# Graph layer on one core: nine batches of edges fetched row by row on two queues, for three on one, with the own side in fp32

## The chip, the cores and the metric

The kernel runs on one core of a Trainium2 chip. The metric is the time of one execution in microseconds; a time stated for a kernel is the median of its runs. Engines are PE (matmul), DVE (VectorE), ACT (ScalarE), POOL (GpSimd) and SP (SyncE, which only issues transfers). ACT and POOL issue transfers of their own too; ACTq, SPq and POOLq in a row stand for such issuing work.

## The reference

A graph layer over 12,500 nodes of 128 features and 412,500 edges, sorted by `dst`, with a residual and a layer norm:

```
theta = x[dst] - x[src]
w = sigmoid(relu(theta @ W1 + b1) @ W2 + b2)
agg = segment_sum(w * theta, dst)
indeg = segment_sum(ones, dst)
out = layernorm(x + agg + indeg * (x @ W4 + b4))
```

## The kernel before

**Tiling.** Edges go through in batches of 7 x 128 (`BT` = 7, `BATCH` = 896), four batches to a chunk (`NB` = 4), 112 chunks, so 448 batches and one short last one. A chunk's edges all end in one window of 128 nodes. A prologue of about 195 us builds `table` in HBM, whose row for a node is 1 KB: `x @ W1` and `x` side by side; it also turns the lists of edges into `src_at` (the source of each edge, edge `p, t` of a batch in partition `p`) and `rel` (the node of the window to which it belongs).

**The source side.** For most batches POOL gathers the rows of `table` by an indirect DMA for each tile of 128 edges, seven a batch, into one of `RB` = 6 slots of `arena` (L783). 21 batches, the first of each fifth chunk, are *held*: POOL loads their rows of `x` in the prologue (L768) and PE projects them in small steps in the 20 batches before (L631, L644). Three batches are *fetched by hand*: `hand_row(g)` gives, from batch 40 on, one row `p` of 7 edges to each batch, ACT loads the 7 numbers into registers (L891) and issues 7 transfers of one 1 KB row each (L895) into `hand_x`. POOL gathers nothing for held and hand batches (24 of them) and goes straight on to the next of the other 425 (`ringed`). Before a batch it waits until its slot has been read (`scaled`) and until PE has done the own side of the batch two before.

**The own side.** PE forms `x[dst] @ W1 + b1` from the window: a one-hot matrix `hot_ne` (ACT: `away` L875, `hot_ne` L883) times the window's projection (L794). It works in bf16: the projection is split on DVE and ACT into three bf16 parts (`high` L910, `take_high` L1044, `mid` L914, `low` L1048), SP writes the parts to HBM (L672) and loads for each batch the 126 rows of 42 near nodes x 3 parts (`parts`, L666). In the prologue DVE works out where these 42 nodes lie (`near_lin`, `near_row`, `neg_ids`), with a round trip through HBM (`near_of`).

**A batch in the main loop.** DVE: `difference` (L998, subtracts the source side in PSUM), `weigh` (L1004), `one_hot_rows` (L1017), `add_logit` (L1012), `scale_rows` (L1027). ACT: `gate` (two sigmoids, L902, L904), the hand row, then `distance` and `one_hot` for batch g + 3. PE: `own_side(g + 2)`, then `add_up(g)` (7 matmuls of 128x130 fp32, L812), with small work in between. Once a chunk: `project_window` (L820), `take_window`, `take_sums`, `finish_rows`, `normalise`, and on SP `load_window` (L690, L691) and `store_result` (L699). The order is written by hand: each engine runs its own loop over the batches, and semaphores tie the loops together. The PSUM of the own side is double (`ps_z`), and the hot matrices and scaled rows are kept for `SB` = 3 batches.

## Time and profile before

| | |
|---|---|
| median of 3 runs | 3931.7 us (3930.0 to 3933.57) |
| the profiled execution | 3929.44 us, its span 3927.6 us |
| granted TensorE clock, mean | 0.619 of full speed |
| POOL busy | 2953.8 us, 75% |
| DVE busy | 2979.7 us, 76% |
| PE busy | 2018.4 us, 51% |
| ACT busy | 1255.4 us, 32% |
| DMA engines, mean busy share | about 0.5, 147 GB/s |

Busy time does not count the work of issuing: on POOL, an indirect DMA counts while its descriptors are written, and the gap to the next one does not; on ACT, register loads and transfers of single rows count as idle ("issue"); SP has no busy time at all. So the share of busy time says little here, and the gaps and what ends them say more.

### The profile page before, as it was taken

The page shows a single profiled execution, that of the slowest core. Times are in us where ns is not written, and L with a number is a line of the kernel's source. Part 1 is how long each engine was busy: PE and PEld are TensorE (multiplying, and loading weights), DVE is VectorE, ACT ScalarE, POOL GpSimd, SP SyncE. Part 2 cuts the span into 40 slices and gives each one's busy share as a digit, 9 for nine tenths or more (in the row PEclk, how much of TensorE's full clock was granted, in tenths as well). Part 3 has the DMA queues.
Part 4 walks back from the last instruction along what each step waited for, and adds up shares of the span by engine and source line. Part 5 has one row for each costly group of instructions (what it writes and reads, how often), then busy time and mean ns, then how long its engine had stood idle before and what let it go on. Part 6 is the DMA issues. An engine that isn't in the chain of part 4 may idle for free.

```text
span 3927.6 us, 48444 instructions
## 1 busy us (share of the span) xinstructions
PE 2018.4 (51%) x10531; PEld 1781.0 (45%) x10531; DVE 2979.7 (76%) x4855; ACT 1255.4 (32%) x2220; POOL 2953.8 (75%) x3123
## 2 busy tenths in 40 slices
PE   3245555555545555555555555555555555555554
PEld 2244444444444444444444444444444444444444
DVE  7568777777777777777777777778778777777777
ACT  1223333333333333333333333333333333333332
POOL 7777777777777777777777777777777777777776
PEclk5565665566666556665666656666666665665666
DMA  7445455555555555555555545555555555555553
GB/s 234 131 138 148 144 147 143 146 147 147 147 147 147 147 147 148 146 148 147 147 147 143 148 145 147 147 146 148 148 146 147 147 148 145 146 148 144 149 147 105
DMA packets 343028, 577.99 MB, mean 147 GB/s; under 512 B 127642, under 2 KB 216768, under 8 KB 342501
## 3 DMA queue, kind: packets, MB, share of 16 engines
q0 software_dynamic: 147264, 399.12, 36.0%
q10 hardware_dynamic: 49501, 110.40, 8.7%
q1 hardware_dynamic: 145970, 65.36, 6.2%
q8 instruction: 87, 1.43, 0.1%
q14 instruction: 206, 1.69, 0.1%
HBM read 549.00 MB, written 31.99 MB: 148 GB/s over the span
## 4 chain that ended last, share of the span: by engine, by line
POOL 60%; issue 24%; DVE 8%; ACTq 4%; ACT 2%; DMA 1%; PE 0%; POOLq 0%; DVEq 0%
POOL arena L783 56%; POOL held_x L768 4%; ACTq L895 3%; DVE logit L1012 2%; DVE diff L1004 2%; DVE ps_both L998 1%; DMA arena<-table,lists 1%; ACT away L875 1%; ACTq L891 1%; DVE edge_rows L1027 1%; DVE edge_rows L1017 1%; ACT hot_ne L883 0%; ACT ps_log L902 0%; DVE square L976 0%; DVE rstd L978 0%
## 5 line engine op out<-in xcount | busy, mean ns | idle before, releaser
L783 POOL DMA_INDIRECT arena<-table,lists x2970 | 2810.2, 946 | 905.0 <-issue 899.5
L875 ACT ACTIVATE away<-dst_rows,neg_ids 126x896 bf16<-126x896 bf16 (+1 forms) x449 | 466.4, 1039 | 1587.6 <-issue 1587.6
L812 PE MATMUL ps_win<-edge_rows 128*128 128x130 f32 x3140 | 716.3, 416 | 424.7 <-DVE edge_rows L1027 406.7
L812 PE MATMUL ps_sum<-edge_rows 128*128 128x130 f32 x3136 | 713.4, 415 | 422.2 <-DVE edge_rows L1027 404.3
L812 PEld LDWEIGHTS ps_win<-edge_rows 128*128 128x128 f32 x3140 | 663.2, 319 | 482.8 <-issue 482.6
L812 PEld LDWEIGHTS ps_sum<-edge_rows 128*128 128x128 f32 x3136 | 660.1, 318 | 480.2 <-issue 479.6
L998 DVE TENSOR_TENSOR ps_both<-ps_both,arena 128x896 f32<-128x896 f32 x425 | 467.0, 1099 | 485.6 <-DMA arena<-table,lists 482.0
L794 PE MATMUL ps_both<-parts,hot_ne 126*128 126x128 bf16 x3138 | 334.3, 266 | 958.7 <-ACT hot_ne L883 633.7
L794 PEld LDWEIGHTS ps_both<-parts,hot_ne 126*128 126x128 bf16 x3138 | 245.9, 118 | 1072.1 <-issue 569.7
L1027 DVE TENSOR_TENSOR edge_rows<-arena,ps_log 128x896 f32<-128x896 f32 x425 | 461.5, 1086 | 129.2 <-ACT ps_log L902 129.0
L1004 DVE SCALAR_TENSOR_TENSOR diff<-ps_both,w_rows 128x896 f32<-128x896 f32 (+1 forms) x449 | 489.4, 1090 | 15.4
L1017 DVE TENSOR_TENSOR edge_rows<-ps_log,lists 128x896 f32<-128x896 f32 (+1 forms) x449 | 484.8, 1080 | 0.0
L1012 DVE TENSOR_REDUCE logit<-diff 128x7 f32<-128x896 f32 (+1 forms) x449 | 482.3, 1074 | 0.0
L883 ACT ACTIVATE hot_ne<-away,ones_col 126x896 bf16<-126x896 bf16 (+1 forms) x449 | 467.1, 1040 | 43.2 <-ACT away L875 1.5
L902 ACT ACTIVATE ps_log<-logit,b_col 128x7 f32<-128x7 f32 (+1 forms) x449 | 120.4, 268 | 900.1 <-DVE logit L1012 899.6
L768 POOL DMA_INDIRECT held_x<-in_x,held_at x147 | 143.1, 973 | 50.0 <-issue 47.6
L1048 DVE TENSOR_TENSOR stage<-rest,stage 128x128 bf16<-128x128 f32 x112 | 32.8, 292 | 167.2 <-ACT stage L914 166.8
L904 ACT ACTIVATE edge_rows<-logit,b_col 128x7 f32<-128x7 f32 (+1 forms) x449 | 130.8, 291 | 0.1
L976 DVE SCALAR_TENSOR_TENSOR square<-rstd,neg_half 128x1 f32<-128x1 f32 x336 | 74.5, 222 | 12.0
L644 PE MATMUL ps_hid<-w,held_xT 128*128 128x128 f32 x294 | 71.4, 383 | 0.0
L644 PEld LDWEIGHTS ps_hid<-w,held_xT 128*128 128x128 f32 x294 | 66.5, 306 | 0.0
L978 DVE SCALAR_TENSOR_TENSOR rstd<-square,rstd 128x1 f32<-128x1 f32 x336 | 54.1, 161 | 11.5
(136 smaller groups left out, 1198.6 us busy)
## 6 DMA issues: line engine op xcount, KB each, us to landing
dst_rows<-rel_of ACTq DMA_DIRECT2D x224, 441.0 KB
arena<-table,lists POOLq DMA_INDIRECT x2970
held_x<-table ACTq DMA_DIRECT2D x2688, 1.0 KB
parts<-parts_of SPq DMA_DIRECT2D x449, 31.5 KB
parts_of<-stage SPq DMA_DIRECT2D x112, 96.0 KB, 3.4
winT<-in_x_cols SPq DMA_DIRECT2D x112, 64.0 KB
window<-in_x SPq DMA_DIRECT2D x112, 64.0 KB
out<-yout SPq DMA_DIRECT2D x112, 64.0 KB
```

Source lines behind the costliest of these rows:

```text
L644: last = nc.tensor.matmul(ps_hid[:, (2 + t) * P:(3 + t) * P], held_xT[:, t, :], w14[:, 0:F], start=True, stop=True)
L768: nc.gpsimd.indirect_dma_start(held_x[:, h * BT + t, :], None, x, ids).then_inc(held_in, 16)
L783: nc.gpsimd.indirect_dma_start(gath[:, slot_of(g) + t, :], None, table, ids)\
L794: last = nc.tensor.matmul(ps_z[b][:, t, :], hot_ne[0:WK, b, t * P:(t + 1) * P], parts[0:WK, buf, :], start=True, stop=True)
L812: last = nc.tensor.matmul(ps_sums(c), hot_en[:, b, t, :], scaled_x[:, b, t, :], start=(j == 0 and t == 0), stop=(stop and t == tiles_of(g) ...
L875: nc.scalar.activation(away[0:WK, b, 0:n], dst_rows[0:WK, p % 2, lo:lo + n], ACT.Abs, bias=neg_ids[0:WK, near_no(g):near_no(g) + 1]).then_ ...
L883: nc.scalar.activation(hot_ne[0:WK, b, 0:n], away[0:WK, b, 0:n], ACT.Relu, bias=ones_col[0:WK, :], scale=-1.0).then_inc(hot_ready, 1)
L998: v.tensor_tensor(ps_z[b][:, 0:n, :], ps_z[b][:, 0:n, :], u, ALU.subtract).then_inc(z_read, 1)
L1004: v.scalar_tensor_tensor(diff[:, 0:n, :], ps_z[b][:, 0:n, :], 0.0, w2_rows[:, :].rearrange("p (a f) -> p a f", a=1).to_broadcast([P, n, F] ...
L1012: v.tensor_reduce(logit[:, b, 0:n], diff[:, 0:n, :], AX.X, ALU.add).then_inc(logit_ready, 1)
L1017: v.tensor_tensor(hot_en[:, b, 0:n, :], ps_col.rearrange("p (a n) -> p a n", a=1).to_broadcast([P, n, P]), rel[:, lo:lo + n].rearrange("p ...
L1027: v.tensor_tensor(scaled_x[:, g % SB, 0:n, 0:F], rows, ps_wgt(g).rearrange("p (t a) -> p t a", a=1).to_broadcast([P, n, F]), ALU.mult)\
```

## The change

Three things, which the diff shows in this order.

1. **Nine hand batches.** Batches 92, 135, 178, ... 436 (`92 + 43 m`) are fetched row by row, for 170, 301 and 432. The numbers of a hand batch are first written to HBM (`hand_of`) and loaded as one row of 896 into partition 0 (`hand_at`, two buffers). SP takes edges 0 to 594 of each such batch, 56 in a chunk, in two runs of 28, each with one register load; ACT takes the other 301, 7 a batch in all of the 387 batches from 42 on, in three pieces (2, 2 and 3) ahead of, between and behind `distance` and `one_hot`. `hand_x` becomes double. So POOL gathers 419 batches, for 425.
2. **Windows two chunks ahead.** SP's turn `c` starts when `finish_rows(c - 2)` is done and loads the window of chunk `c + 2`. `window` gets 4 buffers, `winT` 3. Results are stored in turn `c` for chunk `c - 2`. On PE `project_window(c + 2)` moves from the third to the fourth batch of chunk `c`, on DVE `take_window` from there to the first batch of the next chunk.
3. **Own side in fp32.** `hot_ne` and `own` are fp32 and of all 128 nodes; the splitting, `parts`, `near_*` and all that belongs to them go.

```diff
-HAND = 3
-HAND_FROM = 40
+HAND = 9
+HAND_FROM = 42
+SPAN = 43
+ACT_EACH = 7
+SP_ROWS = BATCH - ACT_EACH * SPAN
+SP_FROM = -(-HAND_FROM // NB)
+SP_LOAD = 28
+SP_EACH = 2 * SP_LOAD
 EARLY = 3
 FULL = CHUNK + 102
...
-        self.hand = [HAND_FROM + (P + 2) * (m + 1) + m for m in range(HAND)]
-        assert self.hand[-1] < self.batches and HAND_FROM > self.held[1] and not set(self.hand) & set(self.held)
+        self.hand = [HAND_FROM + SPAN * (m + 1) + 2 * NB - 1 for m in range(HAND)]
+        assert self.hand[-1] < self.batches and not set(self.hand) & set(self.held)
+        assert HAND_FROM > self.held[1] and HAND_FROM + SPAN > self.held[3] and SP_EACH * SPAN >= SP_ROWS * NB and\
+            SP_FROM + -(-HAND * SP_ROWS // SP_EACH) < self.chunks
...
         def hand_row(g):
-            for m, at in enumerate(z.hand):
-                row = g - (z.hand[m - 1] + 2 if m else HAND_FROM)
-                if g < at:
-                    return (m, row) if 0 <= row < P else None
-            return None
+            m, n = divmod(g - HAND_FROM, SPAN)
+            return (m, SP_ROWS + n * ACT_EACH) if 0 <= m < HAND else None
+
+        def sync_rows(c):
+            lo = (c - SP_FROM) * SP_EACH
+            runs = []
+            for m, row in [divmod(n, SP_ROWS) for n in range(lo, lo + SP_EACH) if 0 <= n < HAND * SP_ROWS]:
+                if runs and runs[-1][0] == m and runs[-1][2] < SP_LOAD:
+                    runs[-1][2] += 1
+                else:
+                    runs.append([m, row, 1])
+            return runs
+
+        def hand_free(m):
+            return (z.hand[m - 2] if m >= 2 else z.held[2 * m + 1]) + 1
+
+        def hand_numbers(kind, m, row, n):
+            return nc.values_load_multi_w_load_instructions(
+                hand_at[0:1, m % 2, row:row + n], engines=[kind], min_val=0, max_val=z.nodes - 1,
+                skip_runtime_bounds_check_because="src holds numbers of nodes")[1]
+
+        def hand_transfer(eng, m, row, number):
+            p, t = divmod(row, BT)
+            eng.dma_start(hand_x[p:p + 1, m % 2, t, :], table[bass.ds(number, 1), :])\
+                .then_inc(hand_in[2 * m + row % 2], 16)
 
...
-        def load_parts(sp, g, row):
-            buf = g % (2 * NB)
-            sp.dma_start(parts[0:WK, buf, :], parts_of[chunk_of(g) % SLOTS, bass.ds(row, WK), :])\
-                .then_inc(parts_in[buf], 16)
-
...
+        def load_window(sp, c, base):
+            sp.dma_start(winT[:, c % 3, :], x_cols[:, bass.ds(base, P)]).then_inc(window_in[c % 4], 16)
+            sp.dma_start(window[:, c % 4, :], x[bass.ds(base, P), :]).then_inc(window_in[c % 4], 16)
+
...
             sp.wait_ge(y_ready, c + 1)
             if c:
                 sp.wait_ge(y_out[(c - 1) % 2], 16 * ((c - 1) // 2 + 1))
             sp.sem_inc(sp_gate, 1)
-            base = clamped(base_i, c, c + 1, z.last_base)[0]
             sp.dma_start(out[bass.ds(base, P), :], yout[:, c % 2, :]).then_inc(y_out[c % 2], 16)
+
+        def store_numbers(sp):
+            sp.wait_ge(src_ready, 1)
+            sp.sem_inc(sp_gate, 1)
+            for m, g in enumerate(z.hand):
+                lo = first_tile(g)
+                sp.dma_start(hand_of[m, :].rearrange("(p t) -> p t", t=BT), src_at[:, lo:lo + BT])\
+                    .then_inc(hand_of_out, 16)
+            sp.wait_ge(hand_of_out, 16 * HAND)
+            sp.sem_inc(sp_gate, 1)
+            for m in range(2):
+                load_numbers(sp, m)
+
+        def load_numbers(sp, m):
+            if m >= 2:
+                sp.wait_ge(scaled, hand_free(m))
+                sp.sem_inc(sp_gate, 1)
+            sp.dma_start(hand_at[0:1, m % 2, :], hand_of[m:m + 1, :]).then_inc(hand_at_in[m % 2], 16)
+
+        def fetch_by_sync(sp, m, row, n):
+            if row == 0:
+                sp.wait_ge(scaled, hand_free(m))
+                sp.wait_ge(hand_at_in[m % 2], 16 * (m // 2 + 1))
+                sp.sem_inc(sp_gate, 1)
+            for k, number in enumerate(hand_numbers(mybir.EngineType.SP, m, row, n)):
+                hand_transfer(sp, m, row + k, number)
 
...
-            for c in range(last_chunk + 1):
-                if c < last_chunk:
-                    store_parts(sp, c + 1)
-                if c:
-                    store_result(sp, c - 1)
-            store_result(sp, last_chunk)
+            store_numbers(sp)
+            for c in range(1, last_chunk):
+                wait(sp, rows_done, c - 1)
+                sp.wait_ge(win_ready, c)
+                sp.sem_inc(sp_gate, 1)
+                lo, hi = max(c - 2, 0), min(c + 2, last_chunk)
+                bases = dict(zip(range(lo, hi + 1), clamped(base_i, lo, hi + 1, z.last_base)))
+                if c + 2 <= last_chunk:
+                    load_window(sp, c + 2, bases[c + 2])
+                for m in range(2, HAND):
+                    if c == hand_free(m) // NB + 2:
+                        load_numbers(sp, m)
+                rows = sync_rows(c)
+                for m, row, n in rows[:1]:
+                    fetch_by_sync(sp, m, row, n)
+                if c >= 2:
+                    store_result(sp, c - 2, bases[c - 2])
+                for m, row, n in rows[1:]:
+                    fetch_by_sync(sp, m, row, n)
+            bases = clamped(base_i, last_chunk - 2, last_chunk + 1, z.last_base)
+            for c in range(last_chunk - 2, last_chunk + 1):
+                store_result(sp, c, bases[c - last_chunk + 2])
             for q in range(2):
                 sp.wait_ge(y_out[q], 16 * len(range(q, last_chunk + 1, 2)))
...
             def own_side(g):
-                b, buf = g % 2, g % (2 * NB)
+                b, c = g % 2, chunk_of(g)
                 wait(pe, relu_ready, g - 1)
-                pe.wait_ge(parts_in[buf], 16 * (g // (2 * NB) + 1))
+                pe.wait_ge(own_ready, c + 1)
                 pe.wait_ge(hot_ready, g + 1)
                 for t in range(tiles_of(g)):
-                    last = nc.tensor.matmul(ps_z[b][:, t, :], hot_ne[0:WK, b, t * P:(t + 1) * P],
-                                            parts[0:WK, buf, :], start=True, stop=True)
+                    last = nc.tensor.matmul(ps_z[b][:, t, :], hot_ne[:, b, t * P:(t + 1) * P], own[:, c % 2, :],
+                                            start=True, stop=True)
                 last.then_inc(z_ready, 1)
 
...
@@ -846,7 +828,7 @@
                 c, j = chunk_and_place(g)
                 if g + 2 < all_batches:
                     own_side(g + 2)
-                if j == 2 and c + 2 <= last_chunk:
+                if j == 3 and c + 2 <= last_chunk:
                     project_window(c + 2)
                 add_up(g)
                 if j == 1 and c:
...
-                nc.scalar.activation(hot_ne[0:WK, b, 0:n], away[0:WK, b, 0:n], ACT.Relu, bias=ones_col[0:WK, :],
+                nc.scalar.activation(hot_ne[:, b, 0:n], away[:, b, 0:n], ACT.Relu, bias=ones_col[:, :],
                                      scale=-1.0).then_inc(hot_ready, 1)
 
-            def fetch_hand(m, row):
-                if row == 0:
-                    act.wait_ge(scaled, (z.hand[m - 1] if m else z.held[1]) + 1)
+            def load_hand(m, row):
+                if row == SP_ROWS:
+                    act.wait_ge(scaled, hand_free(m))
+                    act.wait_ge(hand_at_in[m % 2], 16 * (m // 2 + 1))
                     act.sem_inc(act_gate, 1)
-                lo = first_tile(z.hand[m])
-                ids = nc.values_load_multi_w_load_instructions(
-                    src_at[row:row + 1, lo:lo + BT], engines=[mybir.EngineType.Activation], min_val=0,
-                    max_val=z.nodes - 1, skip_runtime_bounds_check_because="src holds numbers of nodes")[1]
-                for t in range(BT):
-                    nc.scalar.dma_start(hand_x[row:row + 1, t, :], table[bass.ds(ids[t], 1), :])\
-                        .then_inc(hand_in[2 * m + t % 2], 16)
+                return hand_numbers(mybir.EngineType.Activation, m, row, ACT_EACH)
+
+            def fetch_hand(m, row, numbers, part):
+                lo, hi = part * ACT_EACH // 3, (part + 1) * ACT_EACH // 3
+                for k in range(lo, hi):
+                    hand_transfer(nc.scalar, m, row + k, numbers[k])
 
...
-                    mid(c + 1)
                 gate(g)
-                if g == 0:
-                    high(1)
-                if j == 3 and c + 2 <= last_chunk:
-                    high(c + 2)
-                if hand_row(g):
-                    fetch_hand(*hand_row(g))
+                by_hand = hand_row(g)
+                if by_hand:
+                    numbers = load_hand(*by_hand)
+                    fetch_hand(*by_hand, numbers, 0)
                 if g + 3 < all_batches:
                     distance(g + 3)
+                if by_hand:
+                    fetch_hand(*by_hand, numbers, 1)
+                if g + 3 < all_batches:
                     one_hot(g + 3)
+                if by_hand:
+                    fetch_hand(*by_hand, numbers, 2)
                 if g % DB == 0 and g + 3 + DB < all_batches:
...
             def take_window(c):
                 dve.wait_ge(win_ready, c + 1)
-                wait(dve, low_ready, c)
-                v.tensor_tensor(own[:, :], ps_window(c)[:, 0:F], b1_rows[:, :], ALU.add).then_inc(own_ready, 1)
+                v.tensor_tensor(own[:, c % 2, :], ps_window(c)[:, 0:F], b1_rows[:, :], ALU.add).then_inc(own_ready, 1)
                 wait(dve, rows_done, c - 2)
                 v.tensor_tensor(lin[:, c % 3, :], ps_window(c)[:, F:2 * F], b4_rows[:, :], ALU.add).then_inc(win_read, 1)
-
-            def take_high(c):
-                dve.wait_ge(high_ready, c + 1)
-                v.tensor_tensor(rest[:, :], own[:, :], stage[:, c % 2, 0, :], ALU.subtract).then_inc(rest_ready, 1)
-
-            def low(c):
-                dve.wait_ge(mid_ready, c + 1)
-                v.tensor_tensor(stage[:, c % 2, 2, :], rest[:, :], stage[:, c % 2, 1, :], ALU.subtract)\
-                    .then_inc(low_ready, 1)
 
...
                 difference(g)
                 weigh(g)
-                if j == 1 and c < last_chunk:
-                    low(c + 1)
                 one_hot_rows(g)
                 add_logit(g)
                 if g == 0:
                     take_window(1)
-                if j == 3 and c + 2 <= last_chunk:
-                    take_window(c + 2)
+                if j == 0 and 0 < c < last_chunk:
+                    take_window(c + 1)
                 if j == 1 and c:
                     take_sums(c - 1)
                 scale_rows(g)
-                if j == 0 and c < last_chunk:
-                    take_high(c + 1)
                 if j == 1 and c:
                     finish_rows(c - 1)
                 if j == 2 and c:
@@ -1147,13 +1097,10 @@
```

In the order of the instructions the change shows at three places. SP, one turn of its loop, of before (about chunk 50; `held_x<-table` is a transfer of one row, as `hand_x` lies in the memory of `held_x`):

```order
L672 DMA parts_of<-stage 128x384 [waits low_ready]
L660 TENSOR_LOAD base_i [waits rows_done,win_ready]
L690 REGISTER_ALU
L690 DMA winT<-in_x_cols 128x128
L691 ISA
L691 DMA window<-in_x 128x128
L660 TENSOR_LOAD near_row [waits parts_out0]
L666 ISA
L666 DMA parts<-parts_of 126x128
...
L660 TENSOR_LOAD base_i [waits y_ready,y_out1]
L699 ISA
L699 DMA out<-yout 128x128
```

SP, one turn of its loop, of the change:

```order
L636 TENSOR_LOAD base_i [waits rows_done,win_ready]
L641 REGISTER_ALU
L641 DMA winT<-in_x_cols 128x128
L642 ISA
L642 DMA window<-in_x 128x128
L443 TENSOR_LOAD hand_at
L449 ISA
L449 DMA held_x<-table 1x256
...
L649 ISA [waits y_ready,y_out1]
L649 DMA out<-yout 128x128
L443 TENSOR_LOAD hand_at
```

The pair of lines L449 stands 28 times behind each load of `hand_at`: 56 transfers of a row take the place of the write of the parts and of four loads of parts.

ACT, one batch of before:

```order
L902 ACTIVATE ps_log<-logit,b_col 128x7 [waits logit_ready,summed]
L904 ACTIVATE edge_rows<-logit,b_col 128x7
L891 TENSOR_LOAD lists
L895 ISA
L895 DMA held_x<-table 1x256
...
L875 ACTIVATE away<-dst_rows,neg_ids 126x896 [waits rows_of_dst_in1,hot_ready]
L883 ACTIVATE hot_ne<-away,ones_col 126x896 [waits away_ready,z_ready]
```

ACT, one batch of the change:

```order
L884 ACTIVATE ps_log<-logit,b_col 128x7 [waits logit_ready,summed]
L886 ACTIVATE edge_rows<-logit,b_col 128x7
L443 TENSOR_LOAD hand_at
L449 ISA
L449 DMA held_x<-table 1x256
...
L857 ACTIVATE away<-dst_rows,minus_row 128x896 [waits rows_of_dst_in1,hot_ready]
L449 ISA
L449 DMA held_x<-table 1x256
...
L865 ACTIVATE hot_ne<-away,ones_col 128x896 [waits away_ready,z_ready]
```

Seven pairs stood ahead of both long activations; two stand ahead of them now, two between and three behind.

## Rows read from the trace of the kernel before

**Rows 1.** Groups of instructions by line: busy us, mean ns | idle before.

```profile
L783 POOL DMA_INDIRECT arena<-table,lists x2970 | 2810.2, 946 | 905.0 <-issue 899.5 <-DVE edge_rows L1027 3.4 <-PE ps_both L794 2.1
L998 DVE TENSOR_TENSOR ps_both<-ps_both,arena 128x896 f32<-128x896 f32 x425 | 467.0, 1099 | 485.6 <-DMA arena<-table,lists 482.0 <-DVE mv L1068 0.6
L875 ACT ACTIVATE away<-dst_rows,neg_ids 126x896 bf16<-126x896 bf16 (+1 forms) x449 | 466.4, 1039 | 1587.6 <-issue 1587.6
L1044 DVE TENSOR_TENSOR rest<-own,stage 128x128 f32<-128x128 f32 x112 | 32.2, 287 | 0.0
L1048 DVE TENSOR_TENSOR stage<-rest,stage 128x128 bf16<-128x128 f32 x112 | 32.8, 292 | 167.2 <-ACT stage L914 166.8
```

**Rows 2.** Line L783 alone: ns min/median/max, start of first and last.

```profile
L783 POOL DMA_INDIRECT arena<-table,lists x2970: 942/946/1062, 194.5 to 3908.5; - x198
```

**Rows 3.** Timeline, prologue: start us, us, engine, line.

```profile
132.56 2.18 POOL L768 DMA_INDIRECT held_x<-in_x,held_at  x1 [0.30 <-issue]
132.57 2.05 DVE L547 TENSOR_SCALAR lists<-arena 117x3584 int32<-117x3584 int32 x1
138.15 3.28 ACT L922 ACTIVATE edge_rows<-arena,row_gap 117x3584 f32<-117x3584 int32 x1 [3.09 <-DVE lists L565]
142.42 3.28 ACT L924 ACTIVATE arena<-lists,row_gap 117x3584 bf16<-117x3584 int32 x1
153.15 3.64 POOL L768 DMA_INDIRECT held_x<-in_x,held_at  x1 [0.30 <-issue]
```

**Rows 4.** The chain that ended last, two landings: start us, us, what.

```profile
1331.39 2.71 DMA arena<-table,lists
...
3897.19 3.60 DMA arena<-table,lists
```

**Rows 5.** Timeline, one batch of ACT, then PE at either clock.

```profile
2510.53 0.29 ACT L904 ACTIVATE edge_rows<-logit,b_col 128x7 f32<-128x7 f32 x1
2512.26 3.09 ACTq L895 DMA_DIRECT2D held_x<-table  x7
2515.45 1.04 ACT L875 ACTIVATE away<-dst_rows,neg_ids 126x896 bf16<-126x896 bf16 x1 [4.63 <-issue]
...
3001.64 3.37 PE L812 MATMUL ps_sum<-edge_rows 128*128 128x130 f32 x14 [3.40 <-DVE edge_rows L1027]
...
3007.02 0.90 PE L794 MATMUL ps_both<-parts,hot_ne 126*128 126x128 bf16 x7 [1.15 <-ACT hot_ne L883]
...
3008.90 2.58 PE L812 MATMUL ps_sum<-edge_rows 128*128 128x130 f32 x14
```

**Rows 6.** Issuing lines of ACT and SP: ns min/median/max each.

```profile
L895 ACTq DMA_DIRECT2D held_x<-table x2688: 231/235/480, 543.9 to 3778.5; - x192
L891 ACTq TENSOR_LOAD <-lists x384: 1131/1736/1815, 542.0 to 3774.6; - x192
L666 SPq DMA_DIRECT2D parts<-parts_of x449: 321/337/843, 160.8 to 3864.5; - x150
L660 SPq TENSOR_LOAD <-base_i x224: 269/440/667, 11.3 to 3923.3; - x112
L660 SPq TENSOR_LOAD <-near_row x113: 274/304/505, 160.1 to 3861.9; - x113
```

**Rows 7.** Timeline of SP: an early transfer, then one turn.

```profile
13.39 10.03 SPq L690 DMA_DIRECT2D winT<-in_x_cols  x1
...
2544.68 0.35 SPq L690 DMA_DIRECT2D winT<-in_x_cols  x1
2545.24 0.75 SPq L691 DMA_DIRECT2D window<-in_x  x1
2546.60 1.97 SPq L666 DMA_DIRECT2D parts<-parts_of  x4
2553.59 0.39 SPq L699 DMA_DIRECT2D out<-yout  x1
```

**Rows 8.** The page, the queue of ACT's transfers: packets, MB, share of 16 engines.

```profile
q10 hardware_dynamic: 49501, 110.40, 8.7%
```

168 lines of the change are left out of this document (37 added, 131 removed).

## The prediction

> **What bounds the kernel now.** I read the groups by line first, for what each engine waits for. On POOL all 2970 gathers of the main loop show 905.0 us of idle time before them, and 899.5 of it is "issue", time in which nothing was waited for; waits for other engines sum to 3.4 + 2.1 us [rows 1]. So POOL never waits, and 75% busy is 100% occupied. The line alone says how even it is: 942, 946 and 1062 ns as least, middle and greatest, the first at 194.5 and the last at 3908.5 us [rows 2]. That is 3714.0 / 2969 = 1.251 us for each gather, 0.946 of work and 0.305 of gap. DVE, the busiest by the page, is the one that waits: 482.0 us for landed gathers [rows 1]. Last the timeline of the prologue, for what can stretch a gather: two of them took 2.18 and 3.64 us while DVE worked through one long list each [rows 3]; the operations of that kind stay in the change.
>
> The span is then: 194.5 us until the first gather of the loop, 3715.0 until the last is issued, and a tail of 3927.6 - 3909.5 = 18.1 us in which it lands and the last batch and chunk are finished.
>
> **Nine hand batches, POOL's side.** Hand batches go from 3 to 9, so six more batches of seven gathers leave POOL: 42 x 1.251 = 52.5 us. This lies wholly on the path, as POOL waits for nothing. It is the only large term of the sum.
>
> **Nine hand batches, ACT's side.** ACT fetched 7 rows in each of 384 batches and does so now in 387: the same work. In the timeline it took from 2510.82, the end of the second sigmoid, to 2515.45 for load and rows, 4.6 us with nothing else on ACT [rows 5]. Now two rows come between `distance` and `one_hot` and three behind; each activation takes 1.04 us and issuing goes on under it, so ACT's turn gets shorter by up to 1.9 us. ACT is not on the path, so I count nothing; if issuing does not overlap, the turn stays as it is, 7.5 us, under the 8.76 us (7 x 1.251) that POOL takes for a batch.
>
> **Nine hand batches, SP's side.** This is the term to watch. SP had next to nothing to do and gets 9 x 595 = 5355 rows, 56 a chunk in 95.6 turns. While hand batches are fetched 43 batches hold one hand and 2.15 held ones, so 43 batches take 39.85 x 8.76 = 349 us, 8.12 a batch and 32.5 a chunk. A turn of SP must stay under that. Its parts:
> - A row: a single-row transfer takes 0.235 us on ACT [rows 6]. SP's loads of parts follow each other by (1.97 - 0.34) / 3 = 0.54 us with 0.337 for the transfer [rows 6, 7], so 0.20 of gap. Together 0.44, times 56 = 24.6 us. The upper end is that a row costs SP what a load of parts does: 56 x 0.54 = 30.4.
> - Two loads of 28 numbers, not in this trace. SP's load of 4 numbers took 0.30 us and of one 0.44 [rows 6], so the count hardly matters; ACT's load of 7 took 1.74. I take 1.0 each, with ends of 0.3 and, if the longest load of four (0.505) is scaled to 28, 3.5: 2.0 us, from 0.6 to 7.0.
> - The rest of the turn: load of bases 0.44, from `winT` to behind `window` and a load 1.92, `out` with its gap 0.6 [rows 6, 7]: 3.0 us.
> Sum 29.6 us, from 28.2 to 40.4, against 32.5. I take 29.6, as SP's own rows are the nearest. Then SP still waits some 3 us in each turn for `rows_done`, and the cost is nothing. The rows of a hand batch are then issued well in time: for batch 92 SP starts behind batch 41 and needs 595 / 56 x 4 = 42.5 batches, so it ends at about 84, and each next batch has half a batch more.
>
> Could SP and ACT hold each other up? The middle one of ACT's 2688 transfers took 0.235 us and the longest 0.48 [rows 6], though SP was issuing in its turns all the while. If each of ACT's 28 rows a chunk held SP up by one whole transfer, that would be 28 x 0.235 = 6.6 us more, 36.2 in all. I take none of it and leave it in the rival. The Trainium skill (Perfetto Trace Analysis, DMA Instruction, HWDGE) says that the block which generates descriptors is shared by the sequencers and locked by one at a time; by that rule the 6.6 us would be the bound, where the rows show hardly a trace of it.
>
> **Windows two chunks ahead.** Four fewer register loads and nothing on the path; before, PE waited for transfers of `parts` only and never for a window. Its worth is slack. Turn `c` can start when DVE is past batch 4(c - 1) + 1, and PE needs the window at batch 4c + 3: six batches, 48.7 us, less a landing of 3.6 [rows 4], 45 us. Past it PE would stop, and with it DVE, and then POOL, which waits for the own side of the batch two before.
>
> **Own side in fp32.** PE: seven bf16 matmuls with their weights took 0.90 us, seven in fp32 of 128x130 took 3.37 at the lower granted clock and 2.58 where it rose [rows 5]. So 1.7 to 2.5 us more a batch. PE's batch is then 3.4 + 3.4 and under 1 us of small work, at most 7.8 us, under 8.12; what hides it is DVE's wait for gathers. On the way to DVE: `own_side(g + 2)` can start when batch g is weighed and `add_up(g - 1)` done, about 3 us into batch g, and ends by 7 us, where DVE needs it only two batches (over 12 us) later. ACT: an activation with an fp32 result took 3.28 us for 3584 columns, with a bf16 result 3.28 too [rows 3], so `hot_ne` costs the same 1.04. DVE: 32.2 + 32.8 us of work and 166.8 us of waiting for ACT's `mid` go [rows 1], off the path. The write of three parts a chunk and their load a batch go too, and with them the wait of PE for `parts`. Nothing of it is on the path: 0.
>
> **Prologue and tail.** The round trip of `near_of` and some ten small DVE operations go, the long operations that stretched gathers stay, and nine small stores of numbers come behind them. POOL waits for none. I take 0, bounds -3 and +5. The tail has no hand batch near (the last is 436 of 448): 0, bounds -1 and +3, as its two own sides are fp32.
>
> **Sum.** 3929.4 (profiled execution) - 52.5 = 3876.9. The median stood 2.3 us above it, so 3879.2. Own range with the small bounds 3870 to 3890.
>
> **Rivals.**
> 1. *POOL starts to wait now and then.* Three of the hand batches lie next to a held one (135 and 136; 178 two behind 176; 436 apart), and DVE then works on two batches without POOL's rows while POOL runs ahead. Counted from the start of the gathers of 137 (0), DVE starts 135 at 8.5 us (134 landed at about 2.3, and a batch of DVE's is about 6.2, five operations of 1.1 and small ones), its weighing lets PE finish the own side of 137 by 8.5 + 7 = 15.5, and POOL asks for it at 17.5. So 2 us are left. For: thin. Against: it is the worst place, and ACT's turn gets shorter. Price: a few us at each of nine batches, up to 30 in all: 3885 to 3910.
> 2. *SP becomes the bound (slower).* It decides once a turn takes more than 32.5 + 45 / 95.6 = 33.0 us, and beyond 33.0 + 52.5 / 95.6 = 33.5 it eats the whole gain. With 0.54 a row the turn is 35.4: (35.4 - 33.0) x 95.6 = +229 us, so 4108. With 40.4 us it would be 4590. For: 28 transfers in a row have never been issued; early in the prologue one transfer took 10.03 us, behind a full queue [rows 7]. Against: the single-row rows of ACT, 0.235 in the middle and 0.48 at most.
> 3. *One DMA engine becomes the bound (slower too).* If single rows all go through the same of the 16 engines, it gets 56 + 28 = 84 rows a chunk. ACT's queue took 8.7% of 16 engines for 49501 packets [rows 8], 5467 us, 0.11 a packet, so 84 rows are 9.3 us or 28% of that engine, beside the 50% of all. That fits. From 0.19 us a row it does not: at twice 0.11, 18.5 + 16.2 = 34.7 us a chunk, +2.2 x 95.6 = +210, 4089. Against: gathers landed in 2.71 us amid ACT's bursts and in 3.60 after the last hand batch [rows 4]. The Trainium skill (DMA: Bandwidth & Descriptors, Why a DMA increments its semaphore by 16 and not by 1) says that such a one-row transfer uses a single engine, the lowest-numbered; no row here shows which.
> 4. *The gathers don't go faster in number.* POOL's spacing could grow with transfers in the queues, by 1.4% to cancel the gain. Against: 946 ns in the middle with the greatest at 1062, with hand rows and without.
>
> **How the numbers follow.** Forecast 0.73. Rival 1 0.09, rival 2 0.10, rival 3 0.04, rival 4 (within 0.2%, 3924 to 3940) 0.04. The range goes from 3868 to 3915, which holds the forecast and rival 1. 0.2% is about what a measurement of this kernel can tell from no change. Faster 0.82, same 0.04, slower 0.14.
>
> **What would show it.** POOL: 2928 gathers on the line, 1.251 us apart, waits still a few us, the last at 3856. SP: a run of 28 rows takes about 12.5 us, and SP still waits for `rows_done` 2 to 4 us a turn; if that wait is gone the second rival is at work, and PE's waits for `winT` show it. DVE still waits for gathers, some hundreds of us; PE busy 55 to 65%. Wrong would be: SP's turn over 33 us, landings well over 4 us, or POOL waiting for PE.

## The result, and the profile after

The changed kernel takes 4156.18 us (median of 4 runs, 4154.75 to 4156.95) where the kernel before takes 3931.09: a ratio of 1.0571, 95% interval 1.0553 to 1.059. It is slower by 5.7% where 3879 us were forecast. The span of the profiled execution went from 3927.6 to 4154.5 us, by 226.9, and the mean granted clock of TensorE rose from 0.619 to 0.774, so PE's clock did not cost this. On the chip of the f runs below the kernel before takes 3940 us in six runs and 3932 in one, and three of the four traces made there have gathers of 949 ns for 946, so each run is compared with runs of the kernel before on its own chip.

The page of the changed kernel: busy times, and the chain that ended last, by engine and by line.

```profile
PE 2145.5 (52%) x13669; PEld 1990.0 (48%) x13669; DVE 2915.8 (70%) x4615; ACT 1235.4 (30%) x1996; POOL 2914.9 (70%) x3081
...
SPq 50%; POOL 22%; issue 21%; ACTq 2%; DVE 1%; DMA 1%; PE 1%; ACT 0%; POOLq 0%; DVEq 0%
SPq L449 28%; POOL arena L765 21%; SPq L443 18%; ACTq L598 2%; SPq L636 2%; POOL held_x L750 1%; SPq L642 1%; SPq L649 1%; DMA arena<-table,lists 1%; SPq L641 1%; PE ps_both L776 1%; DVE diff L975 0%; DVE ps_both L969 0%; ACT arena L596 0%; DVE logit L983 0%
```

POOL's busy time fell as forecast, and yet the span grew: 70% busy is no longer 100% occupied. Half of the chain is now SP's queue. L449 are the single-row transfers (5355 of them), and L443 the register loads ahead of them, which take 18% of the chain.

Who waits: POOL's gathers (busy us, mean ns | idle before), then the waits of POOL, PE, DVE and SP (us in total, times, longest).

```profile
L765 POOL DMA_INDIRECT arena<-table,lists x2928 | 2770.5, 946 | 1171.1 <-issue 869.5 <-PE ps_both L776 295.8 <-DVE edge_rows L998 5.9
...
PE ps_win L802 <- DMA window<-in_x: 433.2, 35, 16.9
PE ps_sum L802 <- DMA window<-in_x: 425.1, 34, 16.9
DVE ps_both L969 <- DMA arena<-table,lists: 381.6, 172, 45.5
POOL arena L765 <- PE ps_both L776: 295.8, 67, 13.8
...
SPq L714 <- DVE y L1024: 387.0, 22, 87.9
```

Beside [rows 1], where POOL waited 2.1 us for PE, it now waits 295.8 us for `ps_both`, the own side. PE in turn waits for `window`, which SP loads. SP waited only 22 times for `rows_done` (L714) in 110 turns, so in most turns it had no slack at that point. A gather still takes 946 ns in the middle [rows 2], 2928 of them:

```profile
L765 POOL DMA_INDIRECT arena<-table,lists x2928: 940/946/1073, 195.5 to 4135.9; - x196
```

Without waits 2927 x 1.251 = 3662 us would lie between the starts of the first and the last; 4135.9 - 195.5 = 3940.4 do. So 279 us of waiting were added and 52.5 us of gathers went, which makes the 226.9 us of the span to within 1 us.

Next the sources of SP's rows and loads (ns min/median/max), those of the loads for one stretch each, then the timeline of SP in the same two stretches.

```profile
L449 SPq DMA_DIRECT2D held_x<-table x5355: 224/228/669, 559.9 to 3983.0; - x199
L443 SPq TENSOR_LOAD <-hand_at x198: 941/5678/6044, 558.0 to 3979.1; - x198
...
L443 SPq TENSOR_LOAD <-hand_at x4: 1646/1761/1939, 2264.4 to 2308.8; - x4
...
L443 SPq TENSOR_LOAD <-hand_at x4: 5678/5893/5951, 2553.8 to 2610.9; - x4
```

```profile
2263.36 0.36 SPq L641 DMA_DIRECT2D winT<-in_x_cols  x1
2263.92 0.42 SPq L642 DMA_DIRECT2D window<-in_x  x1
2266.21 11.42 SPq L449 DMA_DIRECT2D held_x<-table  x28
2277.89 0.38 SPq L649 DMA_DIRECT2D out<-yout  x1
2280.45 11.63 SPq L449 DMA_DIRECT2D held_x<-table  x28
2293.62 0.36 SPq L641 DMA_DIRECT2D winT<-in_x_cols  x1
...
2552.88 0.36 SPq L641 DMA_DIRECT2D winT<-in_x_cols  x1
2553.44 0.35 SPq L642 DMA_DIRECT2D window<-in_x  x1
2559.67 11.42 SPq L449 DMA_DIRECT2D held_x<-table  x28
2571.36 0.38 SPq L649 DMA_DIRECT2D out<-yout  x1
2577.82 11.67 SPq L449 DMA_DIRECT2D held_x<-table  x28
2591.03 0.36 SPq L641 DMA_DIRECT2D winT<-in_x_cols  x1
```

Both turns issue the same things. The runs of 28 rows take the same 11.4 to 11.7 us. What differs is the time ahead of each run, 2 us against 6, in which the 28 numbers are loaded into registers. One turn is 30.3 us long and the next kind 38.2, and a chunk of POOL's takes 32.5. The timeline of PE behind that stretch (start, us, in brackets what it waited for):

```profile
2593.76 1.22 PE L802 MATMUL ps_win<-w,winT 128*128 128x256 f32 x2 [5.37 <-DMA window<-in_x]
...
2633.14 1.22 PE L802 MATMUL ps_sum<-w,winT 128*128 128x256 f32 x2 [14.32 <-DMA window<-in_x]
...
2671.95 1.22 PE L802 MATMUL ps_win<-w,winT 128*128 128x256 f32 x2 [16.21 <-DMA window<-in_x]
```

PE now passes a chunk every 39.4 and 38.8 us, at SP's pace, and stops longer at each window.

The two kinds of turn are not mixed. SP's turns follow each other every 30.3 us while it fetches hand batches 4 and 8, and about every 38.3 us for hand batches 1 to 3 and 5 to 7. In those for batch 0 it needs no more than the short ones and waits in between (30.3 to 35.4 us from one to the next). A table of stretches (from:to, length, then busy us of PE, PEld, DVE, ACT and POOL with their counts, the granted clock, the DMA share, GB/s) shows it; POOL's count is that of its gathers. The first ends before SP has used up its lead, the third lies in the turns for batch 4, the second and fourth in turns of 38.3 us:

```profile
923.00:1268.00 345.00, 202.50 (x1256) 184.38 (x1254) 264.73 (x425) 116.13 (x187) 260.88 (x277) 0.83 0.48 142
1340.00:1685.00 345.00, 159.20 (x1084) 150.21 (x1084) 223.64 (x360) 100.28 (x161) 227.92 (x242) 0.74 0.42 124
2141.00:2444.00 303.00, 180.10 (x1146) 167.06 (x1147) 232.88 (x374) 100.77 (x164) 223.05 (x237) 0.83 0.48 141
2858.00:3204.00 346.00, 156.69 (x1080) 147.82 (x1080) 223.28 (x360) 99.42 (x160) 220.53 (x234) 0.77 0.41 121
```

277 gathers in 345 us are the forecast 1.25 us each (345 / 277 = 1.245). 242 and 234 are one per 1.43 and 1.48 us, and the 237 of the third one per 1.28.

What sets batches 0, 4 and 8 apart? Hand batch `m` begins at row 595 `m` of SP's list, and SP takes 28 rows at a time of the whole list. 28 is a multiple of 4, and 595 `m` is one only for `m` = 0, 4, 8. So the loads of the others begin at a number of `hand_at` that doesn't lie on 16 bytes. That is the theory the runs had to test (theory A): **a register load of 28 numbers that doesn't begin on 16 bytes takes three times as long, and this alone makes the change slower.** Its rivals: the transfers of single rows crowd a queue or one DMA engine (rival 3 of the prediction), so that windows arrive late whatever the loads cost; or the own side in fp32 makes PE late.

### The profile page after: what moved, and what is told of

Read it like the earlier page. It is cut to its first block, busy times and chain, and to the rows that moved or that the text cites. A ratio compares the mean times of both kernels' runs of the same rounds, so it can differ in the third digit from the quotient of the medians.

```text
span 4154.5 us, 68446 instructions
## 1 busy us (share of the span) xinstructions
PE 2145.5 (52%) x13669; PEld 1990.0 (48%) x13669; DVE 2915.8 (70%) x4615; ACT 1235.4 (30%) x1996; POOL 2914.9 (70%) x3081
## 4 chain that ended last, share of the span: by engine, by line
SPq 50%; POOL 22%; issue 21%; ACTq 2%; DVE 1%; DMA 1%; PE 1%; ACT 0%; POOLq 0%; DVEq 0%
SPq L449 28%; POOL arena L765 21%; SPq L443 18%; ACTq L598 2%; SPq L636 2%; POOL held_x L750 1%; SPq L642 1%; SPq L649 1%; DMA arena<-table,lists 1%; SPq L641 1%; PE ps_both L776 1%; DVE diff L975 0%; DVE ps_both L969 0%; ACT arena L596 0%; DVE logit L983 0%
## 5 line engine op out<-in xcount | busy, mean ns | idle before, releaser
L776 PE MATMUL ps_both<-own,hot_ne 128*128 128x128 f32 x6276 | 992.8, 321 | 765.5 <-DVE diff L975 726.2
L776 PEld LDWEIGHTS ps_both<-own,hot_ne 128*128 128x128 f32 x6276 | 913.2, 230 | 831.1 <-DVE diff L975 794.5
L857 ACT ACTIVATE away<-dst_rows,minus_row 128x896 bf16<-128x896 bf16 (+1 forms) x449 | 466.2, 1038 | 886.3 <-issue 886.3
L794 PE MATMUL ps_win<-edge_rows 128*128 128x130 f32 x3140 | 479.4, 314 | 152.9 <-DVE edge_rows L998 147.3
L794 PE MATMUL ps_sum<-edge_rows 128*128 128x130 f32 x3136 | 483.8, 316 | 127.0 <-DVE edge_rows L998 120.7
L794 PEld LDWEIGHTS ps_win<-edge_rows 128*128 128x128 f32 x3140 | 455.7, 226 | 185.6 <-issue 178.4
L794 PEld LDWEIGHTS ps_sum<-edge_rows 128*128 128x128 f32 x3136 | 461.9, 229 | 159.2 <-issue 151.3
L865 ACT ACTIVATE hot_ne<-away,ones_col 128x896 f32<-128x896 bf16 (+1 forms) x449 | 467.1, 1040 | 42.8 <-ACT away L857 0.8
L802 PE MATMUL ps_win<-w,winT 128*128 128x256 f32 x114 | 61.6, 640 | 433.2 <-DMA window<-in_x 433.2
L802 PE MATMUL ps_sum<-w,winT 128*128 128x256 f32 x110 | 58.0, 626 | 425.1 <-DMA window<-in_x 425.1
```

The source lines that it names most:

```text
L776: last = nc.tensor.matmul(ps_z[b][:, t, :], hot_ne[:, b, t * P:(t + 1) * P], own[:, c % 2, :], start=True, stop=True)
L794: last = nc.tensor.matmul(ps_sums(c), hot_en[:, b, t, :], scaled_x[:, b, t, :], start=(j == 0 and t == 0), stop=(stop and t == tiles_of(g) ...
L857: nc.scalar.activation(away[:, b, 0:n], dst_rows[:, p % 2, lo:lo + n], ACT.Abs, bias=minus_row[:, :]).then_inc(away_ready, 1)
L865: nc.scalar.activation(hot_ne[:, b, 0:n], away[:, b, 0:n], ACT.Relu, bias=ones_col[:, :], scale=-1.0).then_inc(hot_ready, 1)
```

## Experiments

All are the changed kernel with the edit shown. The runs f and g are told first, since their times can be compared with those above; the runs e were made on another chip, on which all kernels are slower.

**f1_pad: move the numbers so that every load of 28 begins on 16 bytes.** Nothing else is touched, neither the number of rows nor their order.

```diff
-        hand_at = sb("hand_at", [1, 2, BATCH], I32)
+        hand_at = sb("hand_at", [1, 2, BATCH + 4], I32)
+        def pad_of(m):
+            return SP_ROWS * m % 4
...
-                hand_at[0:1, m % 2, row:row + n], engines=[kind], min_val=0, max_val=z.nodes - 1,
+                hand_at[0:1, m % 2, pad_of(m) + row:pad_of(m) + row + n], engines=[kind], min_val=0, max_val=z.nodes - 1,
...
-            sp.dma_start(hand_at[0:1, m % 2, :], hand_of[m:m + 1, :]).then_inc(hand_at_in[m % 2], 16)
+            sp.dma_start(hand_at[0:1, m % 2, pad_of(m):pad_of(m) + BATCH], hand_of[m:m + 1, :]).then_inc(hand_at_in[m % 2], 16)
```

> The changed kernel with the numbers of hand batch m shifted by 3m mod 4 places in hand_at, so that each of SP's full loads of 28 numbers starts on 16 bytes; nothing else changes. Theory A (a register load that starts off 16 bytes fetches number by number, 5.7 to 5.9 us for 28, where one on 16 bytes takes 1.9): every turn of SP takes 30.3 us of work, under the 32.5 of a chunk, POOL waits a few us in all, 3879 us (3872 to 3890), ratio 0.987. Rival B (rows or queues are slow in six of nine hand batches): 4154 us, ratio 1.057, as the changed kernel.

Measured: 3888.95 us against 3940.29 of before on the same chip, ratio 0.9869 (0.9853 to 0.9886); its profiled execution took 3879.70, the other three 3888.87 to 3889.59. Its own loads, POOL's gathers with what they waited for, and SP's wait for `rows_done` (L717 here):

```profile
L446 SPq TENSOR_LOAD <-hand_at x198: 948/1844/5967, 557.5 to 3663.6; - x198
...
L768 POOL DMA_INDIRECT arena<-table,lists x2928 | 2772.2, 947 | 892.7 <-issue 887.5 <-PE ps_both L779 3.7 <-DVE edge_rows L1001 1.5
...
SPq L717 <- DVE y L1027: 564.2, 66, 88.8
```

The middle load fell from 5678 to 1844 ns, POOL's waits for PE from 295.8 to 3.7 us, and SP waits again (7 of the 198 loads still take over 3 us, up to 5967 ns; they stand where a new hand batch begins, whose first rows lie off 16 bytes by the padding). Four numbers of padding turn +5.7% into -1.3%. Three landings of gathers from the chain that ended last, while SP and ACT both fetch single rows:

```profile
965.11 2.76 DMA arena<-table,lists
...
2008.12 2.88 DMA arena<-table,lists
...
2963.25 5.38 DMA arena<-table,lists
```

The first two are next to the 2.71 us of [rows 4]. The last, and one of 5.35 at 2796.84, are longer than any in the same chain of the kernel before (2.71 to 4.55 us), so it isn't shown that the single rows delay no gather. No delay of theirs reaches POOL, which waits 3.7 + 1.5 us in all. The packets that the trace records fit this: each single row is one packet of 1024 bytes that takes 54 ns in the mean, so 84 rows a chunk are about 4.6 us of an engine's 32.5 if one engine carries them all (which engine does, the trace doesn't say).

**f2_off1: the same buffer, but every load off 16 bytes**, those of batches 0, 4 and 8 too.

```diff
+        def pad_of(m):
+            return (SP_ROWS * m + 1) % 4
```

> The same with one more place of shift, so that every full load of 28 starts one number behind a multiple of four. Theory A: all 95.6 turns take 38.3 us; beyond 33.0 us a turn costs its excess, 95.6 x 5.3 = 507 us over 3877: 4330 to 4390 us, ratio 1.11. Rival B: 4154 us, ratio 1.057.

Measured: 4359.45 us, ratio 1.1065 (1.1046 to 1.1083), 419.2 us over the kernel before on the same chip. Its loads, and POOL's and PE's waits:

```profile
L446 SPq TENSOR_LOAD <-hand_at x198: 1481/5723/6056, 559.5 to 4216.0; - x198
...
PE ps_sum L805 <- DMA window<-in_x: 638.3, 44, 16.7
PE ps_win L805 <- DMA window<-in_x: 637.4, 44, 16.2
```

The 95 turns that fetch rows are 37.7 to 39.2 us long, but for two of 35.2 and 32.2 us, where hand batches 1 and 5 begin and some loads fall on 16 bytes. There is no stretch in which SP catches up. f1 and f2 differ by one number's place in a buffer and by 470 us.

**f3_hand1: windows two chunks ahead and the own side in fp32, but one hand batch instead of nine.**

```diff
-HAND = 9
+HAND = 1
...
-            for m in range(2):
+            for m in range(min(2, HAND)):
```

> The changed kernel with one hand batch (92) in place of nine: windows two chunks ahead and own side in fp32 stay, SP fetches in 10.6 turns only. POOL has 2984 gathers, 14 more than before the change. If the fp32 own side and the windows lie off the path: 3929.4 + 14 x 1.251 = 3947 us profiled, ratio 1.0045, POOL waiting under 15 us. Rival: PE with 14 fp32 matmuls a batch holds POOL up through the own side; then over 3970 us, ratio over 1.010.

Measured: 3957.35 us, ratio 1.0043 (1.0026 to 1.006): +17.1 us on the median before. Two hand batches fewer than before are 14 gathers more, 14 x 1.251 = 17.5 us. (The profiled spans differ by more, 3955.4 - 3927.6 = 27.8 us. The gathers took 949 ns in the trace of f3 and 946 in that of before, and 3 ns x 2984 = 9 us accounts for most of the rest.)

```profile
L765 POOL DMA_INDIRECT arena<-table,lists x2984 | 2832.3, 949 | 910.0 <-issue 883.2 <-PE ps_both L776 23.5 <-DVE edge_rows L998 3.4
```

The 23.5 us put down to `ps_both` are 77 gaps of at most 0.3 us, the usual gap between two gathers. So the own side in fp32 and the new windows together are worth nothing on the path, as forecast, and the rival that PE is late by itself falls. The mean granted clock of this run was 0.83.

**g1_late: windows one chunk ahead again** (SP's turn starts a chunk later), the loads as in the change.

```diff
-                wait(sp, rows_done, c - 1)
+                wait(sp, rows_done, c)
```

> The changed kernel (loads as they are) with SP's turn c starting one chunk later, behind finish_rows(c - 1), so that its lead over the window's deadline is 2 batches less a landing, about 12 us, for 45. Theory (the loss is what the long turns exceed the chunk by, less the lead that is used up first, and the fast stretches win back at most the lead): the first three long hand batches cost 33 us more, the next three lose what a larger lead could win back, 23 - 12 = 11 us: 4154 + 44 = 4198, 4180 to 4215 us, ratio 1.068. Rival (the lead does not matter, SP's rows of the hand batches arrive too late instead and DVE waits for them): 4154 us or a jump of far more.

Measured: 4192.82 us, ratio 1.0661 (1.0643 to 1.0679), 37 us over the changed kernel; POOL waited 334.1 us for `ps_both` (295.8 there). 44 were expected, 33 for the first three long hand batches and 11 for the next three. The trace puts all of it into the first: at 2480 us POOL has issued 1697 gathers for 1727 in the changed kernel, 30 fewer (37 us), and at 3740 us 27 fewer. So the load two chunks ahead does what it is for: it lets SP be late by one chunk of 32.5 us more before PE stops. It lengthens the fuse, once, and doesn't shorten the turn.

**g2_padlate: f1's padding with g1's edit.**

> The shifted version (all full loads on 16 bytes) with SP's turn starting one chunk later. Theory: a turn of 30.3 us fits in 32.5, and its window is loaded at its start, so 12 us of lead are enough: 3879 us, ratio 0.987, POOL waiting under 10 us. Rival: SP's long runs of rows make it late for the window at the chunks with a hand or held batch, where DVE runs faster than POOL: 3900 us or more.

Measured: 3880.86 us against 3932.82, ratio 0.9869 (0.9853 to 0.9886), the same ratio as f1; POOL waited 2.1 us for PE in all. Once the turn fits into a chunk, windows two chunks ahead are worth nothing.

**f4_ten: f1's padding and one hand batch more**, with two more rows in each of ACT's turns.

```diff
-HAND = 9
+HAND = 10
...
-SPAN = 43
-ACT_EACH = 7
+SPAN = 39
+ACT_EACH = 9
```

> The shifted version with ten hand batches: ACT takes 9 edges a batch for 7, a hand batch every 39 batches, 2921 gathers for 2928, SP's turns as before. If only the number of gathers counts once SP keeps up: another 7 x 1.251 = 8.8 us less, 3870 us, ratio 0.9845. Rival: ACT's longer turn (9 rows, a load of 2.1 us) or the 8% more single rows cost as much as they bring: 3879 us or more.

Measured: 3878.71 us, ratio 0.9843 (0.9826 to 0.9859). POOL waited 9.8 us for `ps_both`, 32 gaps of at most 0.3. The median lies 10.2 us under that of f1 on the same chip, where seven gathers fewer are 8.8. The profiled executions seem to say otherwise, 3879.7 for f1 and 3881.0 here, but most gathers start 1.251 us apart in f1's trace and 1.254 in this one, and 0.003 x 2921 = 8.8 us is just what seven gathers fewer save. So the tenth hand batch most likely brings its 8.8 us. It isn't quite shown, as the intervals of the two ratios overlap (0.9853 to 0.9886 for f1). Both beat the kernel before and the changed one.

**g3_loads: what does a register load cost?** The changed kernel, with loads of 1 to 28 numbers behind SP's last store and ACT's last work, two of each form and from different first numbers, each followed by as many single-row transfers into a buffer nobody reads any more.

```diff
+            for _ in range(2):
+                numbers = nc.values_load_multi_w_load_instructions(hand_at[0:1, 0, 1:1+28], engines=[mybir.EngineType.SP], ...
+                for number in numbers:
+                    sp.dma_start(hand_x[at // BT:at // BT + 1, 0, at % BT, :], table[bass.ds(number, 1), :]).then_inc(bench_in, 16)
```

> The changed kernel with a bench at the end of SP's and of ACT's work: loads of n numbers from place o of hand_at, each followed by n row transfers that only keep the registers in use. On SP about 0.33 + 0.22 us for each four numbers on 16 bytes (28 at place 0: 1.9), and 0.32 + 0.20 for each number otherwise (28 at place 1, 2 or 3: 5.9). If ACT's loads follow the same law: 7 at place 1, 2 or 3 1.7 us and 7 at place 0 1.2, so that ACT's 1.74 of before was seven numbers one by one and not ACT's own slowness. If ACT is slower by itself, 7 at place 0 also takes 1.7.

Measured (ns min/median/max of two; the whole run, with the bench in it, 4384.77). SP: four numbers from number 0 (L749) and from 1 (L754), then 28 from 0, 1, 2, 3 and 4 (L784 to L804). ACT: seven numbers from 0 (L1027) and from 1 (L1032):

```profile
L749 SPq TENSOR_LOAD <-hand_at x2: 561/564/567, 4157.0 to 4159.3; - x2
L754 SPq TENSOR_LOAD <-hand_at x2: 1127/1128/1130, 4161.5 to 4164.4; - x2
...
L784 SPq TENSOR_LOAD <-hand_at x2: 1895/1897/1899, 4219.8 to 4233.5; - x2
L789 SPq TENSOR_LOAD <-hand_at x2: 5934/6013/6092, 4247.2 to 4264.8; - x2
L794 SPq TENSOR_LOAD <-hand_at x2: 5923/5929/5935, 4282.5 to 4300.3; - x2
L799 SPq TENSOR_LOAD <-hand_at x2: 5923/5925/5927, 4317.7 to 4335.5; - x2
L804 SPq TENSOR_LOAD <-hand_at x2: 1901/1920/1940, 4353.2 to 4366.6; - x2
...
L1027 ACTq TENSOR_LOAD <-hand_at x2: 1250/1264/1278, 4150.6 to 4155.1; - x2
L1032 ACTq TENSOR_LOAD <-hand_at x2: 1823/1828/1832, 4159.4 to 4164.2; - x2
```

From numbers 0 and 4 a load of 28 takes 1.90 to 1.94 us, from 1, 2 and 3 5.93 to 6.01. On 16 bytes each four numbers more cost (1897 - 564) / 6 = 222 ns; off them each number more costs (5929 - 1128) / 24 = 200 ns. This fits a load that moves four numbers at a time from 16 bytes on and what is left over one by one, and off them all one by one: seven numbers from number 0 took 1.19 and 1.24 us on SP, and the sum is 0.34 + 0.22 + 3 x 0.20 = 1.16. ACT's seven from number 0 took 1.26 and not 1.7, so ACT isn't slower by itself.

**On the slower chip: e1_pad, e2_off1, e3_hand1, e4_loads.** These are f1, f2 and f3 and a bench like g3's (on SP alone). That chip ran every kernel longer, the kernel before at 4734.47 us. In the traces of the e runs the instructions are as long as elsewhere (DVE's operations 1.09 us, gathers 946 to 949 ns, the record of a single-row transfer 228) and the gaps between them are longer: most of SP's runs of 28 rows in e1 took 17 to 30 us, up to 40, instead of 11.3 to 11.9.

> The changed kernel with the numbers of hand batch m shifted by 3m mod 4 places in hand_at, so that each of SP's full loads of 28 numbers starts at a multiple of 4 numbers (16 bytes). Nothing else changes. Theory A (the register load is slow when it does not start on 16 bytes: 5.7 us for 1.7): every turn of SP takes 30.3 us as in the stretches of hand batches 0, 4 and 8, SP waits for finish_rows in each, POOL waits a few us in all, time 3877 + 2 = 3879 us (3872 to 3890). Rival B (the turn is long in six of nine hand batches because rows or queues are slow there, for example one DMA engine taking all single rows): no change, 4154 us, turns of 38.3 us in the same stretches.

Measured: 5803.72 us, ratio 1.2264 (1.2235 to 1.2294).

> The same with one more place of shift, so that every full load of 28 starts one number behind a multiple of 4. Theory A: all 95.6 turns take 38.3 us, so hand batches 0, 4 and 8 become as slow as the rest. From 33.0 us a turn costs its excess: 95.6 x (38.3 - 33.0) = 507 us over 3877, less what is left at the end, so 4330 to 4390 us. Rival B: 4154 us again, with the three fast stretches where they were.

Measured: 6230.7 us, ratio 1.3152 (1.3121 to 1.3184).

> The changed kernel with one hand batch (92) in place of nine: the windows two chunks ahead and the own side in fp32 stay, SP fetches in 10.6 turns only, all of them with loads on 16 bytes. POOL has 425 + 2 batches, 2984 gathers, 14 more than before the change. If the fp32 own side and the new order of the windows lie off the path as predicted: 3929.4 + 14 x 1.251 = 3947 us profiled, 3949 median, ratio to before 1.0045, POOL waiting under 15 us. Rival: PE with 14 fp32 passes a batch holds POOL up through the own side; then over 3970 us and POOL waits for PE by some tens of us.

Measured: 4670.88 us, ratio 0.9872 (0.9852 to 0.9891).

> The changed kernel with a bench behind SP's last store: SP loads n numbers from place o of hand_at and issues a row transfer for each (only to keep the registers in use), twice for each of 18 pairs (n, o). Theory A: cost goes by pieces, where a piece is four numbers on 16 bytes or else one number: 28 at place 0 or 4 about 1.7 us, 28 at place 1, 2 or 3 about 5.7; 4 at place 0 0.3 us, at place 1 to 3 about 1.0; 7 about 1.7 wherever it starts or a little over 1 at place 0. Rival: cost goes by the count alone, 28 the same at all places.

Measured: one run of 6343.67 us with its bench; its loads of 28 took 1.89 to 1.90 us from numbers 0 and 4, and 5.92 to 5.93 from 1, 2 and 3, as in g3.

The order of the first two and the bench are what the loads let expect, but the sizes are not. Where each row costs SP so much more, the turn overruns with the padding too (POOL waited 1549.7 us for `ps_both` in e1), and nine hand batches cost 23%. Rival 2 has then a second way in, which the chip decides and not the kernel. e3 missed too: a ratio of 1.0045 was expected, and with 0.9872 it is 64 us faster than the kernel before, so on this chip the own side in fp32 and the new windows are worth something. Why, and what made that chip slower, stays open.

## Why the prediction was wrong, by its steps

**POOL's side: right.** 2928 gathers of 0.946 us, and with no waits added f1 and g2 end where the sum put them: their medians lie 51.3 and 52.0 us under those of the kernel before on the same chip, for -52.5 forecast. f1 changes only where SP's and ACT's loads begin, so the 52.5 us are real, and the changed kernel lost them and 227 us more.

**SP's side: the step that failed, by one term of its sum.** The turn was put at 29.6 us:
- Rows: 56 x 0.44 = 24.6 forecast; 11.42 + 11.63 = 23.1 measured, 0.41 a row. A little less, not more.
- The rest of the turn: 3.0 forecast; 30.3 - 23.1 - 3.5 = 3.7 measured. The load of bases accounts for it: it reads five numbers for the windows two chunks ahead and takes 1.24 us in the middle (L636: 304/1238/1407 ns), where 0.44 was counted.
- **Two loads of 28 numbers: 2.0 forecast with ends of 0.6 and 7.0; 3.5 measured where they begin on 16 bytes, and 11.8 (two of 5.9) in the six hand batches where they don't.** The step read "the count hardly matters", from loads of 4 and of 1 number on SP, and set aside ACT's 1.74 us for 7 numbers. That row was the nearest in kind. Scaled to 28 it gives 1.74 x 28 / 7 = 7.0 us a load, 14 a turn, 42 in all. Taken as an end, it alone says that the turn can pass 33.0. The end of 3.5 a load that the prediction took instead was the longest SP load of four (0.505, [rows 6]) times seven; 5.9 for 28 numbers off 16 bytes is 11.7 times that row. (Why SP's loads of four took 0.30 in the middle before and 0.56 in the bench stays open.)

The trace of the kernel before already held the answer. [rows 6] gives ACT's loads of seven numbers 1131 ns at least and 1736 in the middle, and split by hand batch they are two groups, not one:

```profile
L891 ACTq TENSOR_LOAD <-lists x256: 1710/1763/1815, 542.0 to 2692.5; - x128
...
L891 ACTq TENSOR_LOAD <-lists x128: 1131/1162/1192, 2721.1 to 3774.6; - x128
```

The first 256 are for batches 170 and 301, whose seven numbers begin 14 and 7 places behind a multiple of 28 in `src_at`; the last 128 are for batch 432, whose numbers begin at a multiple of 28, so on 16 bytes if the tile itself begins there. The sums from the bench, 0.32 + 7 x 0.20 = 1.72 and 1.16 us, meet both.

So the sum was good for a third of the turns (30.3 against 29.6) and 8.6 us short for two thirds. The path from a long turn to a waiting POOL was in the prediction: a turn of 38.3 lies beyond the 33.0 from which rival 2 decides. That the place of the first number sets the cost of a load was not.

**Rival 2: its mechanism held and its price nearly, its chance of 0.10 was too low.** It named the wait (PE for the window), the fuse of 45 us and the price per turn. Its 4108 us lie near the 4156 measured by luck: they come from rows of 0.54 us in all turns, and the rows took 0.41. With 38.3 us in the long turns the price works for this run: hand batches 1 to 3 are 595 x 3 / 56 = 31.9 turns, each 5.8 us over 32.5, 185 us, less the 45 of lead, 140. In the 10.6 turns for batch 4 SP wins 2.2 us each back, 23, and batches 5 to 7 cost 185 - 23 = 162. Together 302 us against 279 measured. f2, where all turns overrun, gives 95.6 x 5.8 - 45 = 509, against 4340.0 - 196.2 - 2927 x 1.254 = 473 us in its trace. Both are too high, by 23 and 36 us; what makes the difference stays open.

**Windows two chunks ahead: right.** "Its worth is slack", one chunk: g1 lost 37 us without it, about a chunk of 32.5, and g2 lost nothing. (Its "four fewer register loads" aren't in the traces: SP's loads of bases went from two a chunk to one, L660 x224 and L636 x112, and the one that is left got longer.)

**Own side in fp32: right.** Nothing on the path (f3, within 1 us of its 14 more gathers). `hot_ne` with an fp32 result took 1.04 us as forecast (L865, 508 to 1045 ns). PE didn't become the bound. By PE's timeline the seven matmuls (two passes each, x14) took 1.80 us where the granted clock was 1.00 and 3.36 where it was 0.50, the latter being the 3.4 that the prediction worked with:

```profile
1005.12 1.80 PE L776 MATMUL ps_both<-own,hot_ne 128*128 128x128 f32 x14 [1.91 <-ACT hot_ne L865]
...
2515.78 3.36 PE L776 MATMUL ps_both<-own,hot_ne 128*128 128x128 f32 x14 [2.89 <-DVE diff L975]
```

**ACT's side: right.** ACT's idle time before `away` fell from 1587.6 us [rows 1] to 886.3, 2.4 us a batch where [rows 5] has 4.63. In the timeline of ACT two rows end before `away` and the next are issued under it:

```profile
2602.64 0.86 ACTq L449 DMA_DIRECT2D held_x<-table  x2
2603.60 1.04 ACT L857 ACTIVATE away<-dst_rows,minus_row 128x896 bf16<-128x896 bf16 x1 [2.38 <-issue]
2603.74 0.62 ACTq L449 DMA_DIRECT2D held_x<-table  x2
```

**Rivals 1, 3 and 4: fell.** In f1 POOL waits 3.7 us for PE in all, 0.3 at most at a time, in hand batches next to held ones too. One DMA engine isn't the bound: rows follow each other at 0.41 us in all turns, one row took an engine 54 ns and not the 0.11 us of the prediction (a mean over ACT's larger packets too), and f1 with the same 84 rows a chunk has no wait from them, though two of its landings took over 5 us. The gather took 946 ns as before, 1.251 from one to the next. And SP and ACT don't hold each other up by 6.6 us a turn: the turn is 30.3 with ACT's transfers in it. The Trainium skill (Perfetto Trace Analysis, DMA Instruction, HWDGE) says that one sequencer at a time has that block; no cost of it is seen here.

**Prologue and tail: right.** The first gather of the loop at 195.5 us (194.5 in [rows 2]); from the start of the last to the end 4154.5 - 4135.9 = 18.6 us, before 3927.6 - 3908.5 = 19.1.

## What to carry to other kernels

When a queue gets a new kind of instruction, price it by the nearest row in kind and scale it by its size, from whichever engine it is, and let that be an end of the range; where its middle and its least are as far apart as here (1736 and 1131 ns), split it before scaling. Ask then at which total the turn passes the period of the loop. Where a sequencer loads several numbers into registers from SBUF, lay them so that each load begins on 16 bytes: it cost a padding of four numbers here, took the changed kernel from a ratio of 1.0571 to 0.9869, and made 470 us between the best and the worst place. A load further ahead buys slack once and never makes up for a turn that is longer than the loop's period, so read the turn first.
